# Laying keys and queries on partitions: 6 copies at a stride of 8 become 12 copies onto 8 neighbouring partitions

## The reference

```
q = norm(x) @ wq + bq;  k = ctx @ wk + bk;  v = ctx @ wv + bv     # (self attention: rotated q and k, causal)
p = softmax(q k^T / sqrt(8) + mask)                               # per head, 256 x 256
x = x' + (p v) @ wo + bo
```

## Time and profile before

| | us |
|---|---|
| median of 3 runs | 1797.65 |
| lowest and highest run | 1795.26, 1799.02 |
| profiled execution: its own time | 1797.65 |
| profiled execution: span of the core | 1795.6 |
| PE busy | 1403.7 (78%) |
| DVE busy | 1238.8 (69%) |
| ACT busy | 918.2 (51%) |
| mean granted TensorE clock | 0.877 of 2.4 GHz |

### The profile page before, as it was taken

The page is one execution under the profiler, slowest core; times in us unless marked ns, Lnnn a source line. Parts: engine busy times, 40 slices in busy tenths (PEclk is TensorE's granted clock), DMA queues, the critical chain, the costliest instruction groups (busy, mean ns, idle before and its releaser), DMA issues. The chain is left out here.

```text
span 1795.6 us, 31792 instructions
## 1 busy us (share of the span) xinstructions
PE 1403.7 (78%) x10666; PEld 853.3 (48%) x10666; DVE 1238.8 (69%) x4823; ACT 918.2 (51%) x2002; POOL 338.6 (19%) x360
## 2 busy tenths in 40 slices
PE   5998979962865769994455799999983995778984
PEld 2454434441753534442244456666652884444442
DVE  7888469965347768997666676777765224659987
ACT  4564357641322346655622587777761442127766
POOL 3320012112533135300021000000002333302200
PEclk9999999985997779996577899999995997669996
DMA  3210012111661012200010000000003573002200
GB/s 129 68 42 2 0 25 54 37 36 50 171 137 27 12 53 62 60 6 20 1 61 1 13 7 11 9 7 7 1 1 109 165 199 95 27 18 54 54 2 24
DMA packets 59361, 83.41 MB, mean 46 GB/s; under 512 B 8065, under 2 KB 46209, under 8 KB 58689
## 3 DMA queue, kind: packets, MB, share of 16 engines
q1 hardware_dynamic: 54208, 71.15, 13.2%
q0 software_dynamic: 4992, 10.23, 2.9%
HBM read 51.18 MB, written 9.18 MB: 34 GB/s over the span
## 5 line engine op out<-in xcount | busy, mean ns | idle before, releaser
L872 ACT ACTIVATE L_xattn_probs<-ps 128x1024 f32<-128x1024 f32 x192 | 196.6, 1024 | 101.1 <-PE ps L1065 99.6
L713 DVE TENSOR_REDUCE maxs<-ps 128x4 f32<-128x1024 f32 x128 | 156.5, 1223 | 15.3 <-PE ps L1041 14.1
L3499 ACT ACTIVATE wide_pr<-wide_sc,wide_nm 128x256 f32<-128x256 f32 x256 | 127.0, 497 | 13.3 <-DVE wide_nm L3427 12.7
L1081 PE MATMUL ps<-L_xattn_probs,values 128*32 128x256 f32 x1536 | 122.1, 391 | 1.7 <-ACT L_xattn_qs L944 1.7
L1575 POOL DMA_INDIRECT moe_xs<-normed,moe_table x92 | 87.1, 947 | 155.7 <-PE ps L1605 73.4
L3422 DVE COPY wide_prT<-ps 128x512 f32<-128x512 f32 x64 | 44.2, 691 | 84.4 <-PE ps L3540 84.4
L707 DVE CUSTOM_DVE_ANT_0 L_xattn_masked_scores<-ps,L_xattn_maskQ 128x256 bf16<-128x256 f32 x256 | 93.2, 420 | 9.8 <-PE ps L1041 8.7
L3397 DVE CUSTOM_DVE_ANT_0 wide_sc<-ps,wide_mask 128x256 f32<-128x256 f32 x256 | 93.3, 419 | 3.3 <-PE ps L3525 2.2
L1041 PE MATMUL ps<-keys,L_xattn_qs 64*128 64x256 bf16 x768 | 75.3, 274 | 22.3 <-DVE maxs L713 11.4
L2004 DVE SCALAR_TENSOR_TENSOR moe_z_sb<-ps,moe_wt,moe_a_sb 128x256 f32<-128x256 f32 x46 | 22.3, 484 | 93.7 <-ACT moe_a_sb L2035 93.7
L707 DVE CUSTOM_DVE_ANT_0 L_attn_masked_scores<-ps,L_attn_maskQ 128x128 bf16<-128x128 f32 (+1 forms) x256 | 76.0, 353 | 3.9 <-PE ps L1041 3.7
(11 more groups left out here) (629 smaller groups left out, 3632.8 us busy)
## 6 DMA issues: line engine op xcount, KB each, us to landing
moe_wt<-in_packed_experts SPq DMA_DIRECT2D x23, 707.0 KB, 4.3
moe_wt<-in_packed_experts SPq DMA_DIRECT2D x23, 384.0 KB, 3.8
keys<-L_xattn_k_parts SPq DMA_DIRECT2D x54, 128.0 KB, 2.6
L_xattn_qs<-L_xattn_q_parts SPq DMA_DIRECT2D x54, 128.0 KB, 2.4
expert_out<-moe_y SPq DMA_DIRECT2D x46, 128.0 KB, 1.8
weights<-in_packed_L_xattn SPq DMA_DIRECT2D x2, 1316.0 KB, 7.1
keys<-L_attn_k_parts SPq DMA_DIRECT2D x18, 128.0 KB, 2.6
L_attn_qs<-L_attn_q_parts SPq DMA_DIRECT2D x18, 128.0 KB, 2.4
```

The lines of the kernel that those rows point to most:

```text
L713: v.tensor_reduce(nm, ps[:, BANK_M:BANK_M + 2, :].rearrange("p j (t n) -> p j t n", t=2), AX.X, ALU.max, negate=True).then_inc(S("m_used"), 1)
L872: a.activation(probs[:, s % RING, :, :, :].rearrange("p j t n -> p j (t n)"), ps[:, BANK_P:BANK_P + 2, :], ACT.Exp, scale=HD ** -0.5)\
L1081: mm = pe.matmul(ps[32 * j:32 * j + 32, BANK_V, q0:SEQ], V[:, m % 2 * PT + 2 * b + kt, (g % GROUPS) * 4 + j, :], probs[:, (2 * g + j // 2) ...
L3499: ins = a.activation(pr[:, s % 3, j, qt, :], sc[:, s % 2, j, qt, :], ACT.Exp, bias=nm[:, s % 2, n:n + 1], accum_out=sums[:, s % 2, n:n + 1])
```

## The change

The rows are put in another order. Before, a feature's six rows lay together and one row kind was spread over all partitions at a stride of 8. Now one row kind's 8 features lie together: in each half of 64 partitions, row kind `slot` has partitions 8 slot to 8 slot + 7, and the extra rows are 48 to 63. The contraction sums the same products.

With that, a copy of one row kind has to write two separate ranges, so it is issued as two: each reads 64 partitions and writes 8 neighbouring ones, 64 KB. A pair's keys take 12 copies in place of 6 and so do its queries; over four sublayers and three pairs 144 copies become 288, with the same bytes in all. The counts that `parts_free` and `max_scores` wait for go from 96 to 192 per pair. The two clearing DMAs write partitions 48 to 63 of each half in place of 16 spread ones. The selection matrices at the start, the ones in the keys' second half and the constant `aug` follow the new order.

```diff
--- before.py
+++ after.py
@@ -23,7 +23,7 @@
 GROUPS = 4
 
 Q_PARTS, K_PARTS = (0, 0, 1, 1, 0, 2), (0, 1, 0, 1, 2, 0)
-AUG, STRIDE = len(Q_PARTS), 8
+AUG = 8 * len(Q_PARTS)
 NEG = -1.0e30
 LN_EPS = 1e-5
 ROUND = 1.5 * 2.0 ** 23
@@ -435,7 +435,7 @@
             if m == 2:
                 eng.wait_ge(S(("queries_placed", "keys_placed")[n]), GP)
             elif m > 2:
-                eng.wait_ge(S(("q_laid", "k_laid")[n]), 96 * (m - 2))
+                eng.wait_ge(S(("q_laid", "k_laid")[n]), 192 * (m - 2))
 
         def key_copied(eng, gp):
 
@@ -470,7 +470,9 @@
             if m >= 2:
                 eng.wait_ge(S("p_ready"), WINDOW * (m - 1))
             for part_slot, part in enumerate(K_PARTS):
-                eng.dma_start(kk[part_slot:P:STRIDE, m % 2, :, :], parts(m, 1, part)).then_inc(S("k_laid"), 16)
+                for j in range(2):
+                    r0 = 64 * j + HD * part_slot
+                    eng.dma_start(kk[r0:r0 + HD, m % 2, :, :], parts(m, 1, part)[half[j]]).then_inc(S("k_laid"), 16)
 
         def lay_queries(eng, m):
 
@@ -480,7 +482,9 @@
             else:
                 eng.wait_ge(S("max_in_q"), WINDOW * (m - 1))
             for part_slot, part in enumerate(Q_PARTS):
-                eng.dma_start(qs[part_slot:P:STRIDE, m % 2, :, :], parts(m, 0, part)).then_inc(S("q_laid"), 16)
+                for j in range(2):
+                    r0 = 64 * j + HD * part_slot
+                    eng.dma_start(qs[r0:r0 + HD, m % 2, :, :], parts(m, 0, part)[half[j]]).then_inc(S("q_laid"), 16)
 
         with C.turn() as block:
 
@@ -494,8 +498,8 @@
                 if at + 1 < len(ks):
                     load_weights(C, sp, ks[at + 1], packed)
                 for j in range(2):
-                    r = slice(AUG + j, P, STRIDE)
-                    sp.dma_start(qs[r, 1, :, :], bcast(C.c("zeros").bitcast(BF16)[r], 1, [P // STRIDE, GP, PAIR]))\
+                    r = slice(64 * j + AUG, 64 * j + 64)
+                    sp.dma_start(qs[r, 1, :, :], bcast(C.c("zeros").bitcast(BF16)[r], 1, [64 - AUG, GP, PAIR]))\
                       .then_inc(S("rows_cleared"), 16)
                 if boundary is not None:
                     for m in range(1, PAIRS):
@@ -1028,8 +1032,8 @@
                             pe.wait_ge(S("rotated"), 4)
                     if s % WINDOW == 0:
                         if m:
-                            pe.wait_ge(S("k_laid"), 96 * m)
-                            pe.wait_ge(S("q_laid"), 96 * m)
+                            pe.wait_ge(S("k_laid"), 192 * m)
+                            pe.wait_ge(S("q_laid"), 192 * m)
                         if boundary is not None and s == 0:
                             pe.wait_ge(S("ends_ready"), 1)
                     if s:
@@ -3631,8 +3635,9 @@
         def lay_rows(n, slot):
 
             part = (Q_PARTS, K_PARTS)[n][slot]
-            dst = C.lay[:, n, part, :, :].rearrange("p g (e s) -> p g e s", s=STRIDE)
-            return dst[:, :, :, slot], C.ident.rearrange("p (e g) -> p g e", g=HEADS // 2)
+            dst = C.lay[:, n, part, :, :].rearrange("p g (j r) -> p g j r", r=64)
+            return (dst[:, :, :, HD * slot:HD * (slot + 1)],
+                    C.ident.rearrange("p (j d g) -> p g j d", j=2, d=HD))
 
         with C.turn() as block:
             @block.sync
@@ -3650,13 +3655,13 @@
                 L.tick(g.memset(C.maxs[:], 0.0))
                 L.tick(g.memset(C.values[:, :, :, HD:HD + 1], 1.0))
                 L(g.memset(C.values[:, :, :, HD + 1:32], 0.0))
-                L(g.memset(C.keys[64:128, 1, :, :], 1.0))
+                L(g.memset(C.keys[96:128, 1, :, :], 1.0))
 
             @block.vector
             def _(v):
                 L = Link(v, C.sem("vector_step"))
                 v.memset(C.lay[:, 0, :, :, :], 0.0).then_inc(C.sem("lay_cleared"), 1)
-                L.tick(v.memset(C.keys[0:64, 1, :, :], 1.0))
+                L.tick(v.memset(C.keys[32:64, 1, :, :], 1.0))
                 v.wait_ge(C.const_loaded, 16)
                 v.wait_ge(C.sem("lay_cleared"), 2)
                 L.tick(v.tensor_copy(C.identb[:, :], C.ident))
```

## The result

| | before, us | changed, us |
|---|---|---|
| median (lowest to highest), 10 runs each | 1797.88 (1794.04–1799.63) | 1806.58 (1801.17–1813.70) |
| ratio with 95% interval | | 1.0060 [1.0042, 1.0079] |
| profiled execution, its own time | 1797.65 | 1808.39 |
| span of the core | 1795.6 | 1806.4 |

The change costs some 8 us. The sign, the kind of cause and the first place were as predicted; the forecast of 1865.5 us was nearly eight times too large in the difference (67.9 us against 8.7), and the time lies 1.4 us under its range.

What follows compares the result with a forecast made beforehand. DMA bandwidth as a whole bounded nothing (queue busy 13.2%) and the laying was hidden; 60.4 us of PE waits plus 7.5 of clock made 67.9, on 1797.65 giving 1865.5 us; range 1808 to 1904, likeliest case 1840 to 1904.

Steps and rivals of the forecast that it cites:

- What bounds, and where it first shows: All attention sublayers: laying hidden before; after, PE idles at pair 1's start, 10.3 us late in layer 0's cross attention.
- The issue: SP's queue, each laying: 12 issues at 0.6 us take 7.2 us in place of 3.6; alone they make nothing late.
- The transfer: Laying copies onto 8 neighbouring partitions: engines get in each other's way, 1.2 us per copy, bounded by 0.49 and 2.5.
- the same step once more: Laying copies: twice as many engines on the same memory halve each one's rate, from 14.7 to 7.35 GB/s.
- the prediction's own formula: Keys and queries of one pair pass in order, so the pair is laid 1.9 + 28.8 = 30.7 us after the keys' issue.
- The prediction's rival at 1.0 us per copy: All layings: copies take 1.0 us to issue or move, a laying 12 us; some 21 us lost, 1820 us; chance 0.05.
- A full queue in every laying: Every laying: copies at twice the issue's pace queue up, so a laying of 12 moves for 14.4 us.
- Adding late pairs: Pairs 1 to 3, four sublayers: later issues shift too, so lateness adds: 18.6 + 16.3 + 9.2 + 16.3 = 60.4 us.
- Layer 1 and layer 3: Their cross attentions: layer 1 is late by 9.2 us in sum; layer 3 repeats layer 0's 16.3 us.
- The clock: PE after its waits: granted clock 0.50 costs 0 to 2.9 us; 1.5 for each of five waits over 6 us, 7.5 us.
- The start: Selection matrices' casts on DVE and ACT before the first block: 4.2 us either way at most, taken as 0.
- What would show it: Changed profile: PE idle 8 to 10 us at each pair 1, landing near 8 us, packets near 54208, share some 18%, clock 0.50.

Runs made afterwards that it cites:

- the spread halves: The kernel before with its row order kept, each laying copy split in two by halves of the partitions, 8 partitions at a stride of 8: 1798.67 us, 0.9992.
- over nine: Nine PE waits in the changed kernel with each laying copy issued twice, the second into an unread buffer, except in layer 1's cross attention: 1990.39 us.

## Why the prediction was wrong in size and right in kind

- **What bounds, and where it first shows.** Right. The laying was hidden everywhere, and the first pair to be late is pair 1 of layer 0's cross attention, the one with the largest predicted wait (10.3 us). It waited for 4.3.
- **The issue.** 0.6 us each, hidden: right, the spread halves issue as many and cost nothing (0.9992). In a row they are 0.65 us apart.
- **The transfer.** The direction and the mechanism were right: few neighbouring partitions slow the engines from 16.6 to 7.2 GB/s each in a full queue (I had put 7.35 by "the same step once more"; that it came so close is partly luck, since the share counts 9.1 engines where I had 8). That is 0.99 us per copy against the 1.2 that I took. This was the first step that failed, the price of the transfer. That alternate copies don't overlap was right: issuing one half after the other changed neither the rate nor the time. Set into the prediction's own formula, 1.9 + 24 x 0.99 = 25.7 us from the keys' first issue to PE's start; measured, 286.68 - 262.08 = 24.6 us, predicted 30.7. Put into all the terms of the prediction, 25.7 us (26.9 in layer 1) leave pair 1 late by 3.4, 5.3, 4.0 and 5.3 us and the self attention's pair 3 by 1.4: 19.4 us of waits in place of 60.4. The prediction's rival at 1.0 us per copy had already worked that out to some 21 us, 1820 us (the lateness that it lists adds up to 22 to 24, a slip; redone with its 25.9 it is 20.4).
- **A full queue in every laying.** This was the second step that failed. "The copies queue up: a laying of 12 moves for 14.4 us" was taken for every laying. In the changed kernel the self attention's pair 1 would by 0.99 us be ready at 49.86 + 25.7 = 75.6, after PE's 72.2 (72.97 less the 0.75 gained at the start); PE did not wait, as its copies moved at 96 to 101 GB/s, the pace of the issue. In layer 1 pair 1 would be ready at 687.42 + 26.9 = 714.3, against PE's 710.31; PE did not wait, and the queries moved at 95 GB/s. The slow rate is not a property of the target alone. So 19.4 us of waits became 4.3 to 6.6. In layer 3 a pause of SP seems to keep the queue from filling, but a laying without pause and without a gap moved fast in the self attention; what tips the queue stays open.
- **Adding late pairs.** Wrong mostly by the first step, the price. Pairs 2 and 3 never waited in the changed kernel's profiles; with keys and queries issued further apart in time (291.01 and 304.76 for pair 2 of the cross attention) even 12 copies at 0.99 us are through before the queries come. The prediction had them overlap, since at 1.2 us 14.4 + 1.9 us reach past that gap of 13.75 us.
- **Layer 1 and layer 3.** Layer 1: 9.2 predicted, 0 measured. Layer 3 was said to repeat layer 0, with 16.3 us; its pair 1 waited for 0, 0.22, 2.35 and 0 us.
- **The clock.** Right per wait: 1.5 us were taken, 1.55 lost behind the one wait and at most 1.4 on average over nine. There was one wait instead of five; that 1.5 was hit so closely is luck, since the prediction had chosen it between 0 and 2.9.
- **The start.** Taken as 0 within ±4.2; it gained 0.75 us.
- **What would show it.** Packets unchanged: right. The queue's share: 15.7% against some 18. Half clock behind the wait: right. The landing times could not be read, because the view of the new copies lists none; PE's start stands in for them.

The account for the changed kernel: -0.75 at the start and 4.3 + 1.5 in layer 0's cross attention make 5.0, and layer 3 adds 0 to about 4. That is 5 to 9 us against medians of 7.3 and 8.7. The first profiled execution itself is 10.8 us longer in span. Of that 0.8 were gained ahead of layer 0's cross attention, 5.7 arise in it, 2.9 between 385 and 645 us, where both kernels have the same instructions, 1.4 in layer 1's cross attention, where PE doesn't wait for the laying, and 2.5 in the untouched stretch ahead of layer 3's; what follows is 1.1 shorter. For the stretch from 385 to 645 other profiles show between -1.6 and +3.6, also those of kernels that are as fast as before (+2.7 with a stride of 2), so I count it as scatter. For the 2.5 us ahead of layer 3 that doesn't hold: the kernels as fast as before lie within -0.7 and +0.2. It stays open.

## What to carry to other kernels

Price a transfer in both of its states, at the pace of its issue and in a full queue, and ask for each use which one it is in before adding up waits; one price for all twelve, and that a fifth too high, overstated the loss nearly eightfold. When a layout is free to choose, don't write a DMA's rows to 8 neighbouring partitions: every second one costs no more than every eighth. The wait of 4.27 us in this dense matmul pipeline cost 1.55 us more than it shows, at half the clock.

## What the runs showed of the hardware that I had not expected

- Copies onto 8 neighbouring partitions move at 66 GB/s and a share of 0.57 (7.2 GB/s per busy engine) or at 96 to 101 and 0.43 to 0.45 (14 GB/s), and at times between, in one kernel and with the same instruction.
- A stride of 2 is enough here: 103 GB/s at 0.37, against 103 and 104 at 0.38 with 4 and 8.
- A wait of PE can be exact from run to run (4.24 to 4.28 us) in one sublayer and come and go (0 to 2.35 us) in another with the same instructions.
- Twelve issues by SP took 7.8 to 9.3 us depending on pauses between them.
